# Graph layer on one core: weighted messages, and bucket sums by two rounded products with exact one-hot matrices

## The reference, cut to what matters

```python
x = layernorm(x)                                   # per node
msgs = edge_weight[:, None] * x[dst]               # 200000 x 256
agg = segment_sum(msgs, src, num_segments=12500)
h = (1.0 + eps[0]) * x + agg
h = bn_relu(h @ W1 + b1, g1, be1)                  # and on to a second one,
...                                                # then a gated feed-forward layer
```

## Time and profile before

| | |
|---|---|
| Median of 3 runs | 3713.16 us (3707.75 to 3721.34) |
| The profiled execution | 3724.75 us, span 3722.9 us |
| TensorE busy | 3234.4 us (87%) |
| VectorE busy | 2539.2 us (68%) |
| ScalarE busy | 1211.8 us (33%) |
| GpSimd busy | 775.7 us (21%) |
| HBM | 205 GB/s over the span |

### The profile page before, as it was taken

One profiled execution on the slowest core, in us unless ns is written; L12 is line 12 of the kernel. 1 busy time (PEld: TensorE's weight loads), 2 busy tenths in 40 slices (PEclk: granted clock), 3 DMA queues, 4 the chain that ended last, 5 costly groups with the idle time before them and its releaser, 6 DMA issues. The chain is left out here.

```text
span 3722.9 us, 67093 instructions
## 1 busy us (share of the span) xinstructions
PE 3234.4 (87%) x20000; PEld 2467.0 (66%) x20001; DVE 2539.2 (68%) x6180; ACT 1211.8 (33%) x2051; POOL 775.7 (21%) x730
## 2 busy tenths in 40 slices
PE   2789887888888888699999999897889888849998
PEld 1222213777777777688888888643667667639998
DVE  5877767667666766577777777533777787756665
ACT  2212100555555555300000000046445545443332
POOL 1211100455555555200000000000121222212222
PEclk9555555889888988899999999999999999969999
DMA  2322100777777777799999999500233434256664
GB/s 81 125 85 94 62 0 4 280 282 300 283 290 286 300 290 291 277 330 330 333 330 330 329 330 329 187 0 18 82 122 143 153 137 151 117 208 211 211 210 149
DMA packets 214716, 751.08 MB, mean 202 GB/s; under 512 B 28411, under 2 KB 64549, under 8 KB 189430
## 3 DMA queue, kind: packets, MB, share of 16 engines
q1 hardware_dynamic: 130694, 446.18, 35.2%
q0 software_dynamic: 83952, 304.02, 21.0%
HBM read 411.44 MB, written 353.16 MB: 205 GB/s over the span
## 5 line engine op out<-in xcount | busy, mean ns | idle before, releaser
L1210 PE MATMUL coll_ps_sum<-coll_rows,coll_hot 128*128 128x256 f32 x3724 | 824.1, 380 | 22.1 <-DVE coll_hot L1151 21.9
L1210 PEld LDWEIGHTS coll_ps_sum<-coll_rows,coll_hot 128*128 128x128 f32 x3724 | 700.0, 190 | 117.4 <-DVE coll_hot L1151 23.0
L1151 DVE TENSOR_SCALAR coll_hot<-coll_nodes,coll_rows 128x128 f32<-128x128 f32 x1862 | 495.1, 342 | 229.8 <-PE coll_ps_sum L1210 157.3
L912 PE MATMUL send_ps_msg<-send_window,send_pick 128*128 128x256 f32 x3584 | 576.2, 313 | 19.4 <-ACT send_msg L945 14.1
L945 ACT ACTIVATE send_msg<-send_ps_msg 128x1024 f32<-128x1024 f32 x448 | 454.7, 1024 | 311.7 <-PE send_ps_msg L912 203.2
L793 POOL DMA_INDIRECT messages<-send_msg,send_to x448 | 461.6, 1030 | 431.2 <-ACT send_msg L945 285.9
L912 PEld LDWEIGHTS send_ps_msg<-send_window,send_pick 128*128 128x128 f32 x3584 | 501.4, 210 | 50.4 <-ACT send_msg L945 16.9
L836 DVE TENSOR_SCALAR send_pick<-send_ps_local,edges_down 128x1024 fp32r<-128x1024 f32 x224 | 287.6, 1284 | 254.8 <-PE send_ps_local L899 206.7
L1243 ACT ACTIVATE nodes_hid<-coll_ps_turned 128x256 f32 (+1 forms) x98 | 37.6, 383 | 815.2 <-PE coll_ps_turned L1055 815.2
L537 DVE TENSOR_REDUCE sort_place<-sort_banks 128x8 f32<-128x784 f32 x224 | 193.6, 871 | 115.8 <-PE sort_banks L663 115.8
L2126 PE MATMUL exp_ps_y<-exp_w_hi,exp_hT_hi 128*128 x840 | 246.1, 293 | 0.9 <-DVE exp_hT_lo L2078 0.9
(11 more groups left out here) (298 smaller groups left out, 5207.1 us busy)
## 6 DMA issues: line engine op xcount, KB each, us to landing
coll_rows<-messages SPq DMA_DIRECT2D x98, 1300.0 KB, 7.7
coll_rows<-messages SPq DMA_DIRECT2D x98, 1170.0 KB, 7.6
exp_pay<-regions SPq DMA_DIRECT2D x105, 646.0 KB
send_window<-node_table SPq DMA_DIRECT2D x112, 256.0 KB
node_table<-sort_both SPq DMA_DIRECT2D x25, 1024.0 KB, 4.3
coll_own<-node_table SPq DMA_DIRECT2D x98, 256.0 KB, 4.7
sort_xt<-in_x_dram SPq DMA_DIRECT2D x24, 512.0 KB, 3.8
gate_xt<-in_x_dram SPq DMA_DIRECT2D x24, 384.0 KB
```

The costliest lines, as they stand in the source:

```text
L912: ins = pe.matmul(ps_msg[:, q % 2, a, :], pick[:, q * RUN + a, :], window[:, s, part * D:(part + 1) * D], start=(part == 0), stop=(part == 1))
L1151: ins = dve.tensor_scalar(hot[:, j, :], nodes[:], rows[:, s, j, ROW_ID:ROW_ID + 1], rows[:, s, j, ROW_W:ROW_W + 1], ALU.is_equal, ALU.mult)
L1210: ins = pe.matmul(ps_sum[:, s, 0:D], hot[:, j, :], rows[:, s, j, 0:D], start=(j == 0), stop=(j == CJ - 1))
```

## The change

The edge weight is multiplied into the message's features when they leave PSUM. ScalarE does it for steps 0 to 2, in four pieces of 256 columns because each slot has its own weight per partition; VectorE does step 3 (`keep_last`). The `slot` table no longer repeats a number for each of the five values, and the slot comparison is made once for them.

In the bucket sums `hot` is therefore exact (0 or 1), and fp32r holds it. The features are split: ScalarE makes a rounded copy `high`, VectorE subtracts it for the first tiles of a half and GpSimd for the others, in place (`rest`), and TensorE makes two passes of fp32r matmuls, `hot` x `high` and `hot` x rest. `hot` is made by one comparison a half. Own rows come from a second table `plain`, f32, 1 KB a node, which the sort stage stores too.

```diff
                 def store(i, s):
                     sp.dma_start(chunk(table, i), both[:, s].bitcast(F32)).then_inc(stored[s], 16)
+                    sp.dma_start(chunk(plain, i), xn[:, s]).then_inc(stored[s], 16)
...
                     if later(i, 2):
-                        act.wait_ge(lo_ready, i - 1)
+                        act.wait_ge(stored[s], 32 * before)
...
+                def keep_last(i, s):
+                    dve.wait_ge(gathered, QS * (i + 1))
+                    dve.sem_inc(dve_turn, 1)
+                    dve.tensor_tensor(msg[:, s, QS - 1, :, 0:D], ps_msg[:, (QS - 1) % 2, :, :],
+                                      weight[:, s % 2, (QS - 1) * RUN:QJ].unsqueeze(2).to_broadcast([P, RUN, D]),
+                                      ALU.mult).then_inc(kept_last, 1)
...
                     if not isinstance(i, int) or i + 2 < NG:
                         rows_of(i + 2, s % 2)
+                    if later(i, 1):
+                        keep_last(i - 1, (s - 1) % SLOTS)
                     picks(i, 1)
...
-                    act.activation(msg[:, s, q, :, 0:D], ps_msg[:, q % 2, :, :], ACT.Copy).then_inc(kept, 1)
+                    for a in range(RUN):
+                        ins = act.activation(msg[:, s, q, a, 0:D], ps_msg[:, q % 2, a, :], ACT.Copy,
+                                             scale=weight[:, s % 2, q * RUN + a:q * RUN + a + 1])
+                    ins.then_inc(kept, 1)
...
-                    if later(i, 1):
-                        keep(*prev, 3)
...
-        HALVES = ((0, CA), (CA, CJ))
+        HALVES = ((0, 6, CA), (CA, 15, CJ))
...
+        def rest(eng, s, j0, j1):
+            return eng.tensor_tensor(features(s, j0, j1).bitcast(F32R), features(s, j0, j1), high[:, j0:j1, :].bitcast(F32), ALU.subtract)
...
+                def bucket(b, u, i):                                   # GpSimd
+                    s = u % 2
+                    for h, (j0, jm, j1) in enumerate(HALVES):
+                        pool.wait_ge(high_ready, 2 * b + h + 1)
+                        rest(pool, s, jm, j1).then_inc(rest_pool, 1)
...
-                        for j in range(j0, j1):                        # VectorE
-                            ins = dve.tensor_scalar(hot[:, j, :], nodes[:], rows[:, s, j, ROW_ID:ROW_ID + 1],
-                                                    rows[:, s, j, ROW_W:ROW_W + 1], ALU.is_equal, ALU.mult)
-                        ins.then_inc(hot_ready, 1)
+                        wide = [P, j1 - j0, P]
+                        dve.tensor_tensor(hot[:, j0:j1, :], nodes[:].unsqueeze(1).to_broadcast(wide),
+                                          rows[:, s, j0:j1, ROW_ID].unsqueeze(2).to_broadcast(wide), ALU.is_equal).then_inc(hot_ready, 1)
+                        dve.wait_ge(high_ready, 2 * b + h + 1)
+                        rest(dve, s, j0, jm).then_inc(rest_dve, 1)
                     if later(b, 1):
                         finish(b - 1, 1 - s, 2 * i + (u - 1) // 2 + 1)
...
+                        pe.wait_ge(high_ready, 2 * b + h + 1)          # TensorE
                         for j in range(j0, j1):
-                            ins = pe.matmul(ps_sum[:, s, 0:D], hot[:, j, :], rows[:, s, j, 0:D],
-                                            start=(j == 0), stop=(j == CJ - 1))
+                            pe.matmul(ps_sum[:, s, 0:D], hot[:, j, :], high[:, j, :], start=(j == 0), stop=False)
+                        pe.wait_ge(rest_dve, 2 * b + h + 1)
+                        pe.wait_ge(rest_pool, 2 * b + h + 1)
+                        for j in range(j0, j1):
+                            ins = pe.matmul(ps_sum[:, s, 0:D], hot[:, j, :], features(s, j, j + 1).rearrange("p o f -> p (o f)").bitcast(F32R),
+                                            start=False, stop=(j == CJ - 1))
                         ins.then_inc(added, 1)
                         if h == 0 and later(b, 1):
                             turn(b - 1, 1 - s)
...
                 def bucket(b, u, i):                                   # ScalarE
+                    s = u % 2
+                    for h, (j0, jm, j1) in enumerate(HALVES):
+                        act.wait_ge(rows_in[s][h], 16 * (2 * i + u // 2 + 1))
+                        if later(b, 1):
+                            act.wait_ge(added, 2 * (b - 1) + h + 1)
+                        act.activation(high[:, j0:j1, :], features(s, j0, j1), ACT.Copy).then_inc(high_ready, 1)
+                        if h == 1 and later(b, 1):
+                            keep(b - 1, *((i, u - 1) if u else (i - 1, CH - 1)))
+
+                def keep(b, i, u):
                     act.wait_ge(turned, b + 1)
                     act.activation(place(i, u), turned_sums(u % 2), ACT.Copy).then_inc(kept, 1)
```

More of the change, by code:

```diff
@@ L198, in bucket_pairs, with sort_edges @@
         return self.bucket[:, ds(i, 1), :].rearrange("p o (a u) -> p (o a) u", u=2)
-def sort_edges(nc, c, k, x, src, dst, weight, gnn_eps, table):
+def sort_edges(nc, c, k, x, src, dst, weight, gnn_eps, table, plain):
     with ExitStack() as ctx:
@@ L978, in _, with collect @@
                 keep(NG - 1, SLOTS - 1, TURNS - 1, 2)
-                keep(NG - 1, SLOTS - 1, TURNS - 1, 3)
-def collect(nc, c, src, dst, weight, table, messages, hid):
+def collect(nc, c, src, dst, weight, plain, messages, hid):
     with ExitStack() as ctx:
@@ L986, in collect @@
         rows = m.sb("rows", [P, 2, CJ, ROW])
-        hot = m.sb("hot", [P, CJ, P])
+        high = m.sb("high", [P, CJ, D], F32R)
+        hot = m.sb("hot", [P, CJ, P], F32R)
+        slow_hot = m.sb("slow_hot", [P, GT, P])
         nodes = m.sb("nodes", [P, P])
-        own = m.sb("own", [P, 2, 2 * D])
-        part = m.sb("part", [P, D])
+        own = m.sb("own", [P, 2, D])
         sums = m.sb("sums", [P, 2, D])
@@ L1047, in chunks_in_turn, with own_sum, features @@
             chunk(E - GE, True)
-        def own_sum(dve, steps, s, other, first):
-            steps.link(dve.scalar_tensor_tensor(part[:], own[:, s, 0:D], c.eps1[:, 0:1], first, ALU.mult, ALU.add))
-            return dve.scalar_tensor_tensor(sums[:, other, :], own[:, s, D:2 * D], c.eps1[:, 0:1], part[:], ALU.mult, ALU.add)
+        def own_sum(dve, s, first):
+            return dve.scalar_tensor_tensor(sums[:, s, :], own[:, s, :], c.eps1[:, 0:1], first, ALU.mult, ALU.add)
+        def features(s, j0, j1):
+            return rows[:, s, j0:j1, 0:D]
+        def rest(eng, s, j0, j1):
+            return eng.tensor_tensor(features(s, j0, j1).bitcast(F32R), features(s, j0, j1), high[:, j0:j1, :].bitcast(F32), ALU.subtract)
         def turn_sums(pe, s):
@@ L1076, in bucket @@
                         sp.wait_ge(sums_ready, b - 1)
-                    sp.dma_start(own[:, s, :], table[ds(b * P, P), :]).then_inc(own_in[s], 16)
+                    sp.dma_start(own[:, s, :], plain[ds(b * P, P), :]).then_inc(own_in[s], 16)
                 def slow_bucket(b, u, i):
@@ L1087, in chunk @@
                         if final:
-                            sp.dma_start(own[:, 0, :], table[ds(b * P, P), :]).then_inc(chunk_in, 16)
+                            sp.dma_start(own[:, 0, :], plain[ds(b * P, P), :]).then_inc(chunk_in, 16)
                     chunks_in_turn(sp, chunk)
@@ L1173, in chunk @@
                         for t in range(GT):
[L1174 removed]
+                            ins = dve.tensor_scalar(slow_hot[:, t, :], nodes[:], source[:, t:t + 1], w_col[:, t:t + 1],
                                                     ALU.is_equal, ALU.mult)
@@ L1221, in chunk @@
                         for t in range(GT):
-                            ins = pe.matmul(ps_sum[:, 0, :], hot[:, t, :], gathered[:, t, :], start=(t == 0), stop=(t == GT - 1))
+                            ins = pe.matmul(ps_sum[:, 0, 0:D], slow_hot[:, t, :], gathered[:, t, :], start=(t == 0), stop=(t == GT - 1))
                         ins.then_inc(chunk_sum, 1)
```

84 lines of the change are left out of this document (51 added, 33 removed).

## The result

The changed kernel takes 4088.85 us (4075.61 to 4097.97, 4 runs), the kernel before 3717.25 in the same comparison (3707.75 to 3724.35, 4 runs): ratio 1.0982, 95% interval 1.0946 to 1.1019. The forecast was 4170 us, its range 3890 to 4350. The profiled execution took 4089.42 us around a span of 4087.6, 364.7 over the span before.

The account below looks back on a forecast made before the run. The prediction took TensorE to bound the bucket sums at 8.42 us a bucket, transfers close behind. It summed 3713 + 409 (bucket sums) + 50 (messages) - 3 (sort) = 4169, forecast 4170 us, range 3890 to 4350, the forecast's own 4080 to 4260.

Parts of the forecast that it names:

- The bucket sums: Bucket sums: VectorE and GpSimd exclude each other in a serial cycle of 12.68 us a bucket, +409 us.
- copy to R0: Bucket sums: ScalarE's rounded copy, 2.32 us, and handover, 0.07, before VectorE's first-half subtraction.
- the exclusive stretch: Bucket sums: VectorE's two subtractions and second-half comparison take turns with GpSimd's two subtractions, 8.82 us a bucket.
- the tail: Bucket sums: own-row addition (finish), transposes and ScalarE's keep of the turned sums in series, 1.47 us a bucket.
- The message stage: Message stage: weighted copies on ScalarE and the fourth copy on VectorE cost 0.45 us a group, +50 us.
- The sort stage: Sort stage: extra stores hidden, slot table's four copies shrink to a fifth, -3 us.
- The sum: Whole kernel: median 3713 + 409 + 50 - 3 = 4169 us, forecast 4170; chance 0.60.
- The bounds of the sums: Bucket sums: only exclusive work, 10.3 us a bucket, +184; no overlap and longer handovers, 13.4 us, +488.
- Packed exclusion: Bucket sums: VectorE's second-half operations precede GpSimd's second subtraction; cycle 10.3 to 11.3 us, about 3990 us; chance 0.17.
- Messages in series: Message stage: three longer ScalarE copies form a series with the products, 196 us instead of 50, 4315 us; chance 0.10.
- No exclusion: Bucket sums: VectorE's and GpSimd's subtractions run side by side, cycle 8.3 us, kernel 3700 to 3750 us; chance 0.08.
- TensorE's time was all: Bucket sums: chain looser than read, transfers bound at 7.4 us a bucket, -98 us, 3615 us; chance 0.05.

Follow-up runs that it names:

- 2: Changed kernel with the whole subtraction on VectorE and GpSimd idle in the bucket sums: 3850.83 us, a bucket every 10.49 us.
- 4: Changed kernel with the row of node numbers in PSUM instead of SBUF: 3753.78 us, a bucket every 9.47 us.
- 3: Changed kernel with ScalarE keeping bucket b-2 after the first copy of bucket b: 3875.64 us, a bucket every 10.62 us.
- experiment 8: Changed kernel with node numbers in PSUM, keep of b-2 after the first copy, one tile of each GpSimd part given to VectorE: 3625.01 us, ratio 1.0208.

## Why the prediction was right

**The bucket sums: right, mechanism and size.** Predicted 12.68 us a bucket and +409, measured 12.80 and +420 (on C 12.82 and +424). By the cycle's own steps, from the timeline: copy to R0 2.38 us against 2.39; the exclusive stretch to the start of finish 8.67 against 8.82; from there to the next copy 1.79 against 1.47. The order was another one than assumed: R0, GpSimd, H1, GpSimd, R1, a strict alternation, with R0 first, which starts 0.04 us ahead of GpSimd in each of the 86 buckets. In a cycle of nothing but turns the order changes the sum only by the number of handovers. Part of the closeness is luck, since two errors nearly cancel: the exclusive stretch came out 0.15 shorter than its term and the tail 0.32 longer. The tail was under-sized: the transposes take 0.68 and not 0.44, as at the lower of the two clock levels (1.2 GHz), which the granted clock has from 2015 to 2025 us around the pair in the timeline; it is 0.73 of full in the whole stage, in which TensorE is busy 58%, and the prediction took their duration from a stretch at full clock. That the pair excludes each other was argued from the earlier trace rows; experiments 2 and 4 show it, one by taking GpSimd away, the other by taking one operand out of SBUF; 3 shows that the serial tail counts too, by 2.2 us of the 4.4 that a bucket lost. The gains of 2, 3 and 4 (2.3, 2.2 and 3.3 us) overlap and don't add up: 3 and 4 together, with a tile moved, gave 4.1.

**The message stage: right in size where the stage was full before, wrong where the result was measured.** The term was +50. On C it is +53, of which 46 reach the first load of a bucket. It is made by ScalarE's weighted copies through short waits of TensorE; VectorE's fourth copy, which the term counted in, costs nothing there. On the chip of the result it is -55. The step that failed stands in the row with which it began, "takes 8.05 us for each of 112 groups": I read the 3.6 and 2.6 us in which ScalarE and VectorE idle as the stage's own, although on C the same work takes 6.3 and the rest is waits that no recorded work ends and the lower clock that follows them. That +50 came out on C is thus in part luck: it was sized against idle time which that stage doesn't have. The changed stage loses less in that condition (832 against 762, 70 us) than the kernel before (887 against 708, 178), and so comes out shorter. The clock of 0.89 in the earlier trace rows over a stage in which TensorE does most of the work was the sign that I passed over.

**Sizes within it.** Twelve pieces in a row take 4.53 us (timeline on C), 1.51 a copy, against 1.6 taken. A piece has a median of 0.477 us where 256 elements without the weight take 0.384: 93 ns, as the Trainium skill's page "ScalarE: Activation LUTs", section "What ACT_TABLE_LOAD costs", has it for a pointer operand; the 1.69 a copy that I had worked out from that page was too long. VectorE's fourth copy took 1.22, as priced, the narrow comparison 0.27.

**The sort stage:** -1.6 us on the result's chip and -3.4 on C, against -3. Its DMA share rose from 0.28 to 0.39 under an unchanged stage: hidden.

**The sum.** With the measured terms of C, 3553 + 424 + 46 - 3 = 4020 (46 is the message stage up to the first load of a bucket), against 4017.76 measured. The forecast's own sum of changes, +456, is 468 there; on the result's chip 365, and the message term, 105 us off, is more than the whole of the miss. The bounds of the sums, +184 and +488, were taken from 8.42 us a bucket, the forecast's own +409 from 836 us; on the latter basis they are +175 and +479.

**The rivals.** Packed exclusion: out, 12.80; GpSimd's second subtraction comes between H1 and R1 in each of the 86 buckets, not after R1. Messages in series: out on both chips. No exclusion: out by experiments 2 and 4. TensorE's time was all: out; experiment 8, with most of the exclusion gone, still has 8.70.

**Left open:** what makes the signals of TensorE late on the chips of the result and A and not on B and C; whether it belongs to the chip or to the hour; and why the kernel before suffers from it more (110 such waits and 73 late signals of `sort`, against 30 and 32 in the changed kernel beside it). The mean granted clock doesn't tell it: one execution of the kernel before on C took 3595 us at 0.855, those on A 3698 to 3737 at 0.867 to 0.881. Message packets of 4160 bytes have a median of 162 and 161 ns in the two traces of the kernel before, so each packet is no slower.

## What to carry to other kernels

Moving part of a two-input VectorE operation to GpSimd was a loss here, where both read SBUF: the two take turns, and GpSimd's share costs its own, longer time (2.34 us for 1024 elements, against 1.07 on VectorE). Before the work is split, see whether one operand of the VectorE operation can stand in PSUM: here that one line was worth 3.3 us of a 12.8 us cycle. And where the bounding engine is full at 99% with a second resource at 90%, a cheaper product can return at most the distance between the two, about 1 us of 8.4 here. None of the five versions with the new passes over the same data came below 8.42; the best has 8.70.

Read the granted clock and the regularity of a repeated group before taking its idle time as the stage's own: the same kernel had a stage of 887 us in one trace and 708 in another, and one part of a change was worth -1.8% beside the first and +1.1% beside the second.

## What the runs showed of the hardware

- VectorE and GpSimd took strict turns while both had operations with two SBUF inputs: in all 86 buckets H1 took 3.50 to 3.53 us (1.35 alone) and R1 3.63 to 3.65 (1.49 by its price), and of GpSimd's two subtractions, issued one after the other, the second waited for H1. A tensor_scalar of 128x128 f32 in SBUF was held as well (1.73 in the mean against 0.21).
- With one operand in PSUM, the same comparison ran in 1.35 us inside a GpSimd stretch of 7.50.
- One program took 3732 us on one chip and 3553 on two others; between the traces of such a slower and quicker case the difference lies in a single stage, where the signal of `sort` came up to 3.6 us after the recorded (modelled) end of its matmuls, and 0.01 us after it in the quicker trace. TensorE's granted clock fell after these waits: 29 of 30 stretches at 0.50 began 0.5 to 2.8 us after one had ended.
